# A four-layer graph network on one core: the recurrence keeps twice its state and GpSimd makes the product of z and the state

## The reference

```
A = (adj != 0)
h = x
for l in range(5):
    m = einsum('bnd,de->bne', h, weight[l])
    agg = einsum('bij,bid->bjd', A, m)
    gi = agg @ w_ih.T + b_ih;  gh = h @ w_hh.T + b_hh
    r = sigmoid(i_r + h_r);  z = sigmoid(i_z + h_z)
    n = tanh(i_n + r * h_n)
    h = (1 - z) * n + z * h
x = x + h * mask
```

## Time and profile before

| what | us |
|---|---|
| median of 3 runs | 765.35 |
| profiled execution | 763.7 |
| its span, first to last instruction | 761.9 |
| TensorE busy (matmul) | 695.1 (91%) |
| VectorE busy | 572.2 (75%) |
| ScalarE busy | 547.9 (72%) |
| GpSimd busy | 295.8 (39%) |
| granted TensorE clock, mean | 0.993 |

### The profile page before, as it was taken

One profiled execution on the slowest core, in us unless ns is written; L12 is line 12 of the kernel. 1 busy time (PEld: TensorE's weight loads), 2 busy tenths in 40 slices (PEclk: granted clock), 3 DMA queues, 4 the chain that ended last, 5 costly groups with the idle time before them and its releaser, 6 DMA issues.

```text
span 761.9 us, 12576 instructions
## 1 busy us (share of the span) xinstructions
PE 695.1 (91%) x4198; PEld 588.7 (77%) x4198; DVE 572.2 (75%) x1397; ACT 547.9 (72%) x1147; POOL 295.8 (39%) x423
## 2 busy tenths in 40 slices
PE   3999799989999889989999989989989998989897
PEld 2777588778788778878788777878878877867665
DVE  4688976888877866988967886789876786776343
ACT  4667688578778877667878878667877768657543
POOL 4222525462343353464224433473242333543421
PEclk9999999999999999999999999999999999999999
DMA  6520021100000020300000020210000000210001
GB/s 156 130 69 1 2 58 21 37 2 4 8 1 1 1 59 27 113 29 4 6 4 1 1 59 1 69 44 1 6 6 0 1 1 1 71 42 6 7 1 55
DMA packets 47623, 21.08 MB, mean 28 GB/s; under 512 B 9032, under 2 KB 47560, under 8 KB 47560
## 3 DMA queue, kind: packets, MB, share of 16 engines
q1 hardware_dynamic: 47560, 20.29, 9.9%
HBM read 15.27 MB, written 4.19 MB: 26 GB/s over the span
## 4 chain that ended last, share of the span: by engine, by line
PE 43%; DVE 27%; ACT 15%; POOL 7%; issue 6%; DMA 1%; DVEq 0%; SPq 0%; POOLq 0%; ACTq 0%
PE bank L405 7%; PE bank L406 7%; PE bank L407 7%; PE bank L400 5%; DVE zd L1333 4%; DVE hd L1342 4%; DVE rh L1353 3%; DVE bank L1356 3%; POOL rstd L944 3%; ACT bank L916 2%; ACT xn L713 2%; PE bank L613 2%; DVE h L1337 2%; PE bank L391 2%; PE bank L543 2%
## 5 line engine op out<-in xcount | busy, mean ns | idle before, releaser
L960 POOL TENSOR_TENSOR h_lo<-h,h_hi 128x512 fp32r<-128x512 f32 x64 | 84.2, 1316 | 262.6 <-ACT h_hi L893 262.6
L1353 DVE SCALAR_TENSOR_TENSOR rh<-bank,rh 128x512 f32<-128x512 f32 x80 | 55.0, 688 | 85.4 <-ACT bank L910 84.8
L405 PE MATMUL bank<-h_hi,whh_hi 128*128 128x512 f32 x240 | 105.4, 439 | 11.9 <-DVE rh L1353 11.5
L405 PE MATMUL bank<-g_hi,wc_hi 128*128 128x512 f32 x240 | 104.3, 435 | 0.3
L406 PE MATMUL bank<-g_hi,wc_lo 128*128 128x512 f32 x240 | 95.4, 398 | 0.0
L407 PE MATMUL bank<-g_lo,wc_hi 128*128 128x512 f32 x240 | 95.3, 397 | 0.0
L407 PE MATMUL bank<-h_lo,whh_hi 128*128 128x512 f32 x240 | 95.0, 396 | 0.0
L406 PE MATMUL bank<-h_hi,whh_lo 128*128 128x512 f32 x240 | 95.0, 396 | 0.0
L400 PEld LDWEIGHTS bank<-edge,hn 128*128 128x128 f32 x640 | 84.1, 192 | 8.8 <-DVE edge L1059 1.5
L400 PE MATMUL bank<-edge,hn 128*128 128x128 f32 x640 | 84.7, 275 | 1.2 <-DVE edge L1059 1.2
L713 ACT ACTIVATE xn<-x_res,shift,rstd 128x128 f32<-128x128 f32 x128 | 55.8, 485 | 35.8 <-POOL shift L946 35.8
(11 more groups left out here) (169 smaller groups left out, 1672.5 us busy)
## 6 DMA issues: line engine op xcount, KB each, us to landing
x_in<-in_x SPq DMA_DIRECT2D x8, 512.0 KB, 5.2
adj_in<-in_adj SPq DMA_DIRECT2D x8, 512.0 KB, 4.9
x_res<-in_x SPq DMA_DIRECT2D x16, 256.0 KB, 2.8
out_x<-x_res SPq DMA_DIRECT2D x16, 256.0 KB, 2.3
xz<-x_res SPq DMA_DIRECT2D x16, 50.0 KB
w_sb<-in_L_gnn_W SPq DMA_DIRECT2D x1, 640.0 KB, 5.8
w_sb<-in_L_gnn_W SPq DMA_DIRECT2D x5, 128.0 KB, 5.6
rows<-in_adj SPq DMA_DIRECT2D x32, 0.6 KB
```

The lines of the kernel that those rows point to most:

```text
L405: nc.tensor.matmul(dst[:], w_hi, m_hi, start=start, stop=False)
L960: nc.gpsimd.tensor_tensor(h_lo[q][:], h[q][:], h_hi[q][:].bitcast(f32), ALU.subtract).then_inc(sem["h_lo_new"], 1)
L1353: nc.vector.scalar_tensor_tensor(rh[:], R_BANK[:], 1.0, rh[:], ALU.add, ALU.mult).then_inc(sem["rh_ready"], 1)
```

## The change

The state kept in `h` and `hx` is twice the state. The first state is doubled when it is read (`scale=2.0`), and the weights that meet the state are halved once at the start, as is the mask with which it is added to x. With H = 2h the update reads H = 0.5 * (z' + 1) * H - (z' - 1) * n. GpSimd makes the first product in two operations, `z1` = z' + 1 and `zh` = z1 * H, as soon as z is there; after n, VectorE makes `hd` = (z' - 1) * n and H = 0.5 * zh - hd. The core of the diff:

```
-            "rh_ready", "pre_ready", "n_ready", "hd_ready", "zd_ready",
+            "rh_ready", "pre_ready", "n_ready", "hd_ready", "z1_ready", "zh_ready",
...
                 if n:
-                    pe.wait_ge(sem["h_new"], n)
+                    pe.wait_ge(sem["hd_ready"], n)
                 message_product(I_BANK, 2, layer, True).then_inc(sem["gates_n"], 1)
...
+            def kept_state(n):
+                layer, q = n % STEPS // QUADS, n % QUADS
+                pool.wait_ge(sem["z_ready"], n + 1)
+                if n:
+                    pool.wait_ge(sem["h_new"], n)
+                nc.gpsimd.tensor_scalar(z1[:], gz[n % 2][:], 1.0, None, ALU.add).then_inc(sem["z1_ready"], 1)
+                pool.wait_ge(sem["z1_ready"], n + 1)
+                nc.gpsimd.tensor_tensor(zh[:], z1[:], (h if layer else hx)[q][:], ALU.mult).then_inc(sem["zh_ready"], 1)
+
             def mask_of_round(r):
                 if r:
                     pool.wait_ge(sem["l1_x"], r * QUADS)
+                nc.gpsimd.tensor_copy(half_mask[:], half_mask_all[:, r * RG:(r + 1) * RG])
...
                     low_half(n - 1)
                 beside(2 * n)
+                if n < ALL:
+                    kept_state(n)
                 beside(2 * n + 1)
...
             def new_state(n):
                 layer, q = n % STEPS // QUADS, n % QUADS
+                dve.wait_ge(sem["n_ready"], n + 1)
+                dve.wait_ge(sem["z_ready"], n + 1)
+                nc.vector.scalar_tensor_tensor(hd[:], gz[n % 2][:], -1.0, I_BANK[:], ALU.add, ALU.mult).then_inc(sem["hd_ready"], 1)
                 dve.wait_ge(sem["hd_ready"], n + 1)
-                dve.wait_ge(sem["z_ready"], n + 1)
-                nc.vector.scalar_tensor_tensor(zd[:], gz[n % 2][:], 1.0, hd[:], ALU.add, ALU.mult).then_inc(sem["zd_ready"], 1)
-                dve.wait_ge(sem["zd_ready"], n + 1)
+                dve.wait_ge(sem["zh_ready"], n + 1)
                 if layer == 0 and n >= STEPS:
                     dve.wait_ge(sem["l1_turned"], (n // STEPS - 1) * QUADS + q + 1)
-                nc.vector.scalar_tensor_tensor(h[q][:], zd[:], 0.5, I_BANK[:], ALU.mult, ALU.add).then_inc(sem["h_new"], 1)
-
-            def difference(n):
-                layer, q = n % STEPS // QUADS, n % QUADS
-                dve.wait_ge(sem["n_ready"], n + 1)
-                nc.vector.tensor_tensor(hd[:], (h if layer else hx)[q][:], I_BANK[:], ALU.subtract).then_inc(sem["hd_ready"], 1)
+                nc.vector.scalar_tensor_tensor(h[q][:], zh[:], 0.5, hd[:], ALU.mult, ALU.subtract).then_inc(sem["h_new"], 1)
...
                 if n + 1 < ALL:
                     aggregate_lo(n + 1)
-                difference(n)
                 new_state(n)
```

More of the change, by code:

```diff
@@ L74, in graph_stack @@
         w3T = sb("w3T", [128, 128])
-        mask_all = sb("mask_all", [128, B])
+        mask_all, half_mask_all = sb("mask_all", [128, B]), sb("half_mask_all", [128, B])
         whh_hi, whh_lo = sb("whh_hi", [128, 3, 128], f32r), sb("whh_lo", [128, 3, 128], f32r)
@@ L98, in graph_stack @@
         w3_nat, convT, wihT = adjTI[:, 11, :], adjT[:, 0:LAYERS, :], adjT[:, 5:8, :]
-        mask_r = sb("mask_r", [128, RG])
+        mask_r, half_mask = sb("mask_r", [128, RG]), sb("half_mask", [128, RG])
         deg1, deg3 = sb("deg1", [128, RG]), sb("deg3", [128, RG])
@@ L119, in graph_stack @@
         gz = [sb(f"gz{i}", [128, 512]) for i in range(2)]
-        rh, hd, zd = sb("rh", [128, 512]), sb("hd", [128, 512]), sb("zd", [128, 512])
+        rh, hd, zh, z1 = (sb(i, [128, 512]) for i in ("rh", "hd", "zh", "z1"))
         sT, gate_th, hetS, diff, gated, neg, ex = (sb(n, [128, 512]) for n in
@@ L1138, in _ @@
             nc.vector.tensor_copy(wihT[:], bank[2][:, 0:384].rearrange("e (g c) -> e g c", g=3))
-            nc.vector.tensor_copy(whh_hi[:], bank[3][:, 0:384].rearrange("e (g c) -> e g c", g=3)).then_inc(sem["dve_turns"], 1)
-            nc.vector.tensor_copy(convT[:, 0:4, :], quad(bank[4]))
-            nc.vector.tensor_copy(convT[:, 4, :], bank[5][:, 0:128])
+            nc.vector.tensor_scalar(whh_hi[:], bank[3][:, 0:384].rearrange("e (g c) -> e g c", g=3), 0.5, None,
+                                    ALU.mult).then_inc(sem["dve_turns"], 1)
+            nc.vector.tensor_scalar(convT[:, 0:4, :], quad(bank[4]), 0.5, None, ALU.mult)
+            nc.vector.tensor_scalar(convT[:, 4, :], bank[5][:, 0:128], 0.5, None, ALU.mult)
             nc.vector.tensor_copy(w3T[:], bank[5][:, 128:256])
+            nc.vector.tensor_scalar(half_mask_all[:], bank[5][:, 256:256 + B], 0.5, None, ALU.mult)
             nc.vector.tensor_copy(mask_all[:], bank[5][:, 256:256 + B])
             dve.wait_ge(sem["dve_turns"], 2)
-            nc.vector.tensor_tensor(whh_lo[:], bank[3][:, 0:384].rearrange("e (g c) -> e g c", g=3),
-                                    whh_hi[:].bitcast(f32), ALU.subtract).then_inc(sem["w_turned_read"], 1)
+            nc.vector.scalar_tensor_tensor(whh_lo[:], bank[3][:, 0:384].rearrange("e (g c) -> e g c", g=3), 0.5,
+                                           whh_hi[:].bitcast(f32), ALU.mult, ALU.subtract).then_inc(sem["w_turned_read"], 1)
             nc.vector.tensor_reduce(out=fmax[:], in_=fw[:], op=ALU.max, axis=AX.X, negate=True).then_inc(sem["dve_setup"], 1)
```

4 lines of the change are left out of this document (2 added, 2 removed).

## The result

The changed kernel takes 843.57 us, the median of 4 runs (841.05 to 845.69); on the same chip the kernel before takes 765.47. The ratio is 1.101, with an interval of 1.098 to 1.105. The forecast of 797 had the right side, and was 46.6 us short; 843.6 lies outside the range of 777 to 810. The profiled execution has a span of 839.3 us, 77.4 more than before.

What follows compares the result with a forecast made beforehand. The prediction took TensorE's own queue to set most of the length (busy 618.33 of 660 us). From 763.7 it added 33.2 and took off 1.6, giving 795.3; the median stands 1.65 higher, so 797, range 777 to 810.

Steps and rivals of the forecast that it cites:

- the term of the pair: GpSimd's two new operations a step: 0.8 for z1, 0.1 hand-over, 1.28 for the product; 2.2 us, ends 1.45 and 2.75.
- the forecast's own slope: Width of the range: a pair of 2.75, 0.55 us longer than taken, adds 10 us to the launch.
- steps 26 to 30: Pair queued behind GpSimd's even slot: state 1.65 us later in four steps, 0.9 in step 26; 15.0 over rounds 1 and 2.
- the powers: Pair behind GpSimd's power delays ScalarE's norm: step 33 by 2.2 us in three rounds, step 39 by 2.4 in three.
- the end: End of round 3, where no recurrence hides the late norm: 2.7 us added.
- all the rest: Places with a short queue where TensorE waits on a late VectorE or norm: 1.6 us given back.
- What goes: VectorE loses one operation between n and the state: 0.72 to 0.75 us a step, 57.9 us of busy time.
- An ordinary step: Step 32, no GpSimd queue: pair ends 0.45 us before hd does, and the state starts 0.72 earlier.
- rival 1: VectorE's shorter tail decides: TensorE's 18 waits shrink, 13 us at most, half gives 759; chance 0.09.
- Rival 3: Only the two powers count, the second support's copy finding slack in TensorE's queue: 781 as a median; chance 0.18.
- Two-sided contention: VectorE's two-input SBUF operations held by GpSimd's: costed at nothing, or 2 us a launch under an exclusive lock.
- Rival 4: GpSimd becomes the bound, some 1 us more in each of 60 steps: 857; chance 0.04.

Runs made afterwards that it cites:

- experiment 8: Kernel before, with 24 single GpSimd operations on scratch tiles ahead of its first work, several forms and column counts; only durations are read (launch 775.47 us).
- experiment 9: Changed kernel with z + 1 written as (z + 1) * 1, both arithmetic steps of the operation in use; 797.40 us, ratio 1.041.
- experiment 7: Kernel of experiment 3 with TensorE's n-gate matmul waiting for the new state again instead of hd; 749.83 us, ratio 0.979.
- experiment 3: Changed kernel with VectorE making the product (z' + 1) times the state in one operation before n is awaited, GpSimd's pair gone; 750.54 us, ratio 0.980.
- experiment 6: Changed kernel with GpSimd's product ahead of the even slot's norm and scaling, and without z + 1 (other values); 750.33 us, ratio 0.980.
- experiment 11: Kernel of experiment 3 plus GpSimd's long z + 1 in each step, unawaited save two steps later; 766.82 us, ratio 1.001.
- experiment 2: Changed kernel without z + 1, so the product takes z' itself (other values); 773.04 us, ratio 1.010.
- experiment 5: Changed kernel with z + 1 made by the two-input form, a tile of ones as second operand; 831.02 us, ratio 1.085.
- experiment 12: Kernel of experiment 3 plus GpSimd's short z + 1 in each step, unawaited save two steps later; 756.60 us, ratio 0.988.
- experiment 13: Kernel of experiment 3 plus GpSimd's two-input product in each step, unawaited save two steps later; 778.01 us, ratio 1.016.

## Why the prediction was wrong

The step that failed is the term of the pair, "halfway between is 0.8, which I take". z1 took 1.51, and the upper bound that I gave it, 1.32 of the two-input operation, was no bound: that an operation with fewer inputs is at most as long as one with more was taken for granted, and no row bore it out. The row I put at the lower end, an operation of 16 columns with 279 ns, could not have told: experiment 8 shows that at 16 columns the long and the short form differ by 0.06, at 512 by 0.88. The pair was thus 2.9, outside its ends of 1.45 and 2.75. With the length near the one I had assumed (experiment 9, a pair of 2.0) the kernel takes 797.4. The 769 ns that the prediction cites for a one-input loop of 512 elements fits neither form, with 1.50 and 0.62 measured; the measurement decides.

A second step failed with it: what a longer pair costs. By the forecast's own slope, 10 us for 0.55, a pair of 2.9 gives some 810, not 843.6. The measured slope is 46 us for the 0.88 by which z1 differs between experiment 9 and the changed kernel, 53 us for each us against 18. I had let the length count only where I had found a queue. Of the 42.7 us between the two traces (last two columns below) steps 26 to 30 and 46 to 50, the powers and the end hold 17; the others stand where the forecast had little or nothing: 5 in steps 24, 25, 44 and 45, 5 in round 3, 3 in steps 7 to 10 and 13, and 12 in all the rest.

That the forecast's very number comes out in experiment 9 is partly luck, as the terms show. The growth of each place, from the starts of r in the two timelines (all 80 steps, against before), and what the forecast had:

| place | forecast | after | experiment 9 |
|---|---|---|---|
| steps 24 to 30, and 44 to 50 | 15.0 | 28.9 | 13.1 |
| the same of round 3 | 1.1 | 7.8 | 2.4 |
| steps 7 to 10, round 0 | 0.6 | 4.1 | 1.7 |
| step 13 | 0 | 2.9 | 2.0 |
| steps 33, 53, 73 | 6.6 | 10.9 | 8.1 |
| steps 19, 39, 59 | 7.2 | 12.4 | 9.6 |
| the end | 2.7 | 4.2 | 3.4 |
| all the rest | -1.6 | 6.2 | -5.6 |
| sum | 31.6 | 77.4 | 34.7 |

The forecast's terms for the powers are net: 0.7 and 0.4 were taken off each for what the ordinary steps in front give back, 3.3 us in the six places. In the traces that gain stands in those steps, in the last row but one.

Point by point:

- **What goes**: right in kind. Line 696's wait is worth nothing (experiment 7). VectorE's busy time fell by 49 and not 58. Two thirds of the difference is the last operation, both of whose operands are now in SBUF and which took 762 ns on the mean instead of 687.
- **An ordinary step**: 0.72 earlier was forecast, and it came out at parity (step 34: 0.04 later), because the pair was past the forecast's own margin of 0.45. In experiment 9 the state of step 34 ends 4.32 behind r, 0.71 earlier, as worked out:

```profile
298.56 0.65 ACT L910 ACTIVATE bank<-bank,brz 128x512 f32<-128x512 f32 x1
...
302.19 0.69 DVE L1353 SCALAR_TENSOR_TENSOR h<-zh,hd 128x512 f32<-128x512 f32 x1
```

What that returns was somewhat underrated: 5.6 us in experiment 9 against 4.9 (1.6 and the 3.3 above), and that in a run whose first step began 1.5 us later than before. Experiments 3 and 6 show what the shorter tail is worth where the pair does not take it back, 15 us or 2%; the forecast's rival 1 had 13 at most.
- **Steps 26 to 30**: mechanism and places right. For the 1.65 of the forecast steps 27 to 30 grew by 2.4, 2.4, 3.5 and 2.7, and in experiment 9 by 1.5, 1.5, 2.0 and 1.7. Rival 3, slack in front of the second convolution, is out: line 567 waited 24.4 us.
- **The powers**: step 33 is right once the same is counted on both sides. Without the 0.7 for the step in front the forecast was 2.9 with a pair of 2.2; that gives 2.7 with the pair of 2.0 and 3.6 with that of 2.9, and the step grew by 2.71 (experiment 9) and 3.64. Step 39 was too low by the 0.5 that I let TensorE hide: without it and without the 0.4 the forecast was 3.28, which gives 3.1 and 4.0, and the step grew by 3.11 and 4.04. The power of round 0 (step 13) was counted at nothing, and there was no ground for that: VectorE waited for the product there as in step 33.
- **Forgotten places**: the steps with the zone's norm, which have over 1.2 us of queue, were counted once at 0.9 and else at nothing. With the pair at 2.9 most of them count.
- **Two-sided contention**: costed at nothing. In the changed kernel it is small, since the wait itself keeps VectorE's last operation apart from the pair; in six steps GpSimd's next work holds it, 5.6 us in all. Step 15:

```profile
135.37 1.30 POOL L982 TENSOR_TENSOR adjTI<-adjT,ident 128x512 f32<-128x512 f32 x1
135.52 1.70 DVE L1353 SCALAR_TENSOR_TENSOR h<-zh,hd 128x512 f32<-128x512 f32 x1 [0.69 <-POOL zh L970]
```

VectorE's operation starts 0.15 behind GpSimd's and ends 0.55 after it. “SBUF — State Buffer” of the Trainium skill (section SBUF: two separate sides) calls this an exclusive lock: the operation that starts first has it for its whole length, and the other is fully blocked. The trace agrees for two two-input operations. Beside the long one-input form it does not: VectorE's operation lost 0.44 and ended 0.34 before GpSimd's (experiment 11), and the measurement decides.

- **A cost that I had no term for**: TensorE's clock. The same five steps, from the r of step 28 to that of step 33, before and after:

```profile
core 0: us, PE busy (x) PEld busy (x) DVE busy (x) ACT busy (x) POOL busy (x), PEclk, DMA share, GB/s
232.50:275.90 43.40, 40.09 (x245) 33.84 (x243) 35.80 (x100) 33.90 (x74) 16.24 (x24) 1.00 0.10 26
```

```profile
250.47:302.70 52.23, 45.47 (x247) 38.98 (x246) 30.88 (x95) 33.91 (x73) 30.17 (x34) 0.88 0.08 22
```

Of the 8.8 us by which they grew only 3.4 are idle time of TensorE; 5.4 are busy time at a granted clock of 0.88 (some 12 us of the stretch at the 1.2 GHz level, the rest at 2.4) instead of 1.00. The three falls to the lower level (near 249.0, 269.5 and 283.2) come in, or up to 1.7 us behind, idle times of TensorE of 2.5 to 2.6 us in front of line 567. In the whole span the busy time grew by 21.3, in experiment 9 by 10.7. How much of this lay on the path was not tried.

- **Rival 4**, GpSimd as the bound, had 857, nearer to the measured number than the forecast. Its mechanism did not come: from 20 us to the last step GpSimd is busy for 490 of 733 us, and ordinary steps are at parity.

The range failed for the same two reasons as the number: its upper end rested on a pair of 2.75 and on the slope of 18 us for each us. The chance of 0.85 for slower was well placed.

## What to carry to other kernels

Price an operation by a row of its own form at its own size; a row with more inputs is no upper bound, and a row with few columns tells nothing of the time per column. Before work is given to an engine with idle time, write down what stands in its queue both ahead of the new operations and behind them: each us put into every step of this kernel cost 47 to 59 us in a launch when it was awaited (experiments 2, 5, 9), and 10 to 22 us when nobody waited for it (11 to 13). The places where a queue is seen in the kernel before hold only a part of that (17 of 43 us here), so a longer operation costs more than they tell. And a chain that ends in an awaited value can often be shortened on the same engine, by moving the part that doesn't need the value in front of the wait: that took 2% off with not one operation less.
